# L1 attention with q and k kept transposed, two heads at a time, in a four-layer kernel

## The reference

```python
proj = x @ W_in.T + b_in                       # 256 -> 3 x 16 heads x 64
q, k, v = split(proj)                          # [b, 16, 512, 64] each
q, k = _rope(q, sin, cos), _rope(k, sin, cos)  # lo*cos + hi*sin | hi*cos - lo*sin
att = softmax(causal(einsum('bhqd,bhkd->bhqk', q, k) / 8))
y = einsum('bhqk,bhkd->bhqd', att, v)
return y.reshape(b, t, 1024) @ W_out.T + b_out
```

## Time and profile before

| | us |
|---|---|
| median of 3 runs (lowest to highest) | 2312.48 (2310.83 to 2312.55) |
| the profiled execution, its own time | 2315.66 |
| its span, first to last instruction | 2313.9 |
| PE busy | 1965.5 |
| DVE / ACT / POOL busy | 1723.1 / 1398.9 / 1036.8 |
| L1 attention, its first x transpose to its last update of x | about 949 to 2002 |

### The profile page before, as it was taken

One profiled execution on the slowest core, in us unless ns is written; L12 is line 12 of the kernel. 1 busy time (PEld: TensorE's weight loads), 2 busy tenths in 40 slices (PEclk: granted clock), 3 DMA queues, 4 the chain that ended last, 5 costly groups with the idle time before them and its releaser, 6 DMA issues. The chain is left out here.

```text
span 2313.9 us, 52728 instructions
## 1 busy us (share of the span) xinstructions
PE 1965.5 (85%) x18758; PEld 1405.2 (61%) x18759; DVE 1723.1 (74%) x3717; ACT 1398.9 (60%) x2736; POOL 1036.8 (45%) x1231
## 2 busy tenths in 40 slices
PE   2889989899862999378799999999999999549999
PEld 1666666666561666145577777676767777426665
DVE  4778888788791444468678787879696977679997
ACT  1666666666562444267668696868787878344443
POOL 4435534355014000488747576657575663132222
PEclk9999999999955999689999999999999999869999
DMA  7000000000033332002100000000000000100000
GB/s 241 2 1 2 2 2 2 2 2 2 3 128 127 98 91 79 12 11 35 22 1 2 2 2 2 2 1 2 1 2 2 2 2 2 38 1 14 18 18 23
DMA packets 53114, 57.77 MB, mean 25 GB/s; under 512 B 7121, under 2 KB 47217, under 8 KB 52897
## 3 DMA queue, kind: packets, MB, share of 16 engines
q1 hardware_dynamic: 46240, 45.00, 6.2%
q0 software_dynamic: 6656, 9.85, 2.0%
HBM read 36.22 MB, written 18.61 MB: 24 GB/s over the span
## 5 line engine op out<-in xcount | busy, mean ns | idle before, releaser
L371 PE MATMUL a_bank<-w_in_sb,xnT_sb 128*128 128x512 f16 x1152 | 293.7, 394 | 33.7 <-DVE t_buf_sb L579 26.4
L1116 DVE TENSOR_REDUCE neg_max_sb<-a_bank 128x1 f32<-128x128 f32 (+3 forms) x512 | 236.1, 485 | 92.6 <-PE a_bank L896 88.7
L531 DVE TENSOR_REDUCE neg_max_sb<-a_bank 128x1 f32<-128x128 f32 (+3 forms) x512 | 236.1, 482 | 92.6 <-PE a_bank L288 91.1
L1039 ACT ACTIVATE probT_sb<-a_bank 128x512 f32<-128x512 f32 (+1 forms) x384 | 198.8, 526 | 145.3 <-PE a_bank L919 140.5
L442 ACT ACTIVATE p_hi_sb<-a_bank 128x384 f16<-128x384 f32 (+1 forms) x384 | 205.3, 535 | 120.7 <-PE a_bank L297 119.0
L434 ACT ACTIVATE prob_sb<-a_bank,neg_max_sb 128x128 f32<-128x128 f32 (+3 forms) x512 | 261.4, 543 | 23.9 <-DVE neg_max_sb L531 23.0
L538 DVE TENSOR_TENSOR p_lo_sb<-a_bank,p_hi_sb 128x384 f16<-128x384 f32 (+1 forms) x384 | 228.0, 595 | 59.7 <-ACT p_hi_sb L442 56.1
L453 ACT ACTIVATE stack_sb<-a_bank 128x1024 f16<-128x1024 f16 (+1 forms) x256 | 211.4, 826 | 7.0 <-PE a_bank L342 6.6
L297 PE MATMUL a_bank<-ident_f_sb,prob_sb 128*128 128x128 f32 x1280 | 206.4, 276 | 3.7 <-DVE p_lo_sb L538 3.1
L707 POOL TENSOR_TENSOR rope_w_sb<-t_buf_sb,sin_sb 128x256 f32<-128x256 f32 x128 | 146.0, 1140 | 134.7 <-DVE t_buf_sb L579 132.2
L371 PEld LDWEIGHTS a_bank<-w_in_sb,xnT_sb 128*128 128x128 f16 x1152 | 104.9, 100 | 143.0 <-DVE t_buf_sb L579 34.2
(11 more groups left out here) (268 smaller groups left out, 5613.3 us busy)
## 6 DMA issues: line engine op xcount, KB each, us to landing
sorted_rows<-zeros_sb SPq DMA_DIRECT2D x1, 4992.0 KB, 21.6
x_in_sb<-sorted_rows SPq DMA_DIRECT2D x39, 128.0 KB, 2.1
sorted_results<-y_moe_sb SPq DMA_DIRECT2D x39, 128.0 KB, 1.7
x_sb_sb<-L_attn_x SPq DMA_DIRECT2D x8, 512.0 KB, 10.7
w_raw_sb<-L_ffn_gate_bank SPq DMA_DIRECT2D x8, 512.0 KB, 3.6
w_raw_sb<-L_ffn_up_bank SPq DMA_DIRECT2D x8, 512.0 KB, 4.7
w_raw_sb<-L_ffn_down_bank SPq DMA_DIRECT2D x8, 512.0 KB, 5.8
out<-x_sb_sb SPq DMA_DIRECT2D x32, 128.0 KB, 1.7
```

Of the source, the lines that this page charges most:

```text
L371: last = pe.matmul(out, xnT[:, x, c, j * P:(j + 1) * P], w["in"][:, w_, c, cols], start=k == 0, stop=k == len(terms) - 1)
L531: last = dve.tensor_reduce(neg_max[:, i:i + 1], S[(3 * h + g) % 2][:, off:off + L], AX.X, ALU.max, negate=True)
L1039: act.activation(probT[:, (h // 4) % 2, h % 4, T_AT[r]:T_AT[r + 1]], ST[(3 * h + r) % 2][:, 0:T_AT[r + 1] - T_AT[r]], ACT.Exp).then_inc(s_ ...
L1116: last = dve.tensor_reduce(neg_max[:, h % 2, i:i + 1], S[(3 * h + g) % 2][:, off:off + L], AX.X, ALU.max, negate=True)
```

## The change

`attention` is replaced for L1 by `attention1`. The q and k products are made transposed (weights stationary, tokens moving), so that a unit of 128 rows holds one pair of heads: head 2p in rows 0 to 63, head 2p+1 in rows 64 to 127. What follows from it:

- No stack transposes and no copies of them (342, 453). A fill `qk` is six matmuls of 512 columns, 16 a batch; with 8 `V` fills there are 24 such fills, as before.
- Scores are three products of 64 rows a head (high\*high, high\*low, low\*high) in place of two of 128; those of the two heads alternate, one head writing to bank `S[0]`, the other to `S[1]`. The masks stay products over 128 rows.
- The rotation needs rows exchanged in blocks of 32. SP does it with four SBUF-to-SBUF transfers a pair (`t_buf` to `t_swapped`, 128 KB in all). ACT adds the bias (q and k), DVE makes the cosine part straight from PSUM, POOL the sine part, the sum and the low part, ACT the high part.
- The output projection uses float16 parts: 24 matmuls of 256 columns each in place of eight in float32; DVE makes the low part of yT.
- 24 slots a batch, each with one group of both heads of a pair, and other lags and orders (below). `scores` waits for the exp of both heads of the slot before.

```diff
-LAGS = ((2, 2, 3, 4, 0, 1), (2, 2, 3, 4, 0, 1))
-PE_ORDER = ("STFP", "STPF")
-ACT_ORDER = ("HEW", "PHWE")
-DVE_ORDER = ("OMNWL", "OLWMN")
+AT1 = (tuple(3 * p - 6 for p in range(HEADS // 2)), tuple(3 * p - 5 for p in range(HEADS // 2)),
+       (1, 7, 8, 9), (16, 18, 19, 21), (10, 12, 13, 15), (27, 28, 29, 29), 0)
...
+    LAG_T, LAG_HI, LAG_LO, LAG_PV = 1, 1, 1, 2
+    LAG_WA, LAG_WV, LAG_VH, LAG_VL = 1, 1, 1, 2
+    LAG_W, LAG_ZH, LAG_ZL = (3, 2), (4, 3), (4, 3)
+    LAG_OUT = LAG_PV + 3
+    AT_Q, AT_K, AT_V1, AT_V0, AT_XT, AT_PROJ, YT_LAG = AT1
...
+        out += [("yT", 0, c) for c in range(CHUNKS) if k == 3 * c + LAG_OUT + (c == 0)]
...
+        def scores(b, p, g):
+            G = count(b, 2 * p, g)
...
+            wait(pe, s_exp, G)
+            for i in GROUP_TILES[g]:
+                L = (i + 1) * P
+                for n, (q, k) in enumerate(((z_hi, z_hi), (z_hi, z_lo), (z_lo, z_hi))):
+                    for a in range(2):
+                        rows = slice(a * DH, (a + 1) * DH)
+                        pe.matmul(S[a][:, off:off + L], q[rows, at_q, i * P:(i + 1) * P], k[rows, at_k, 0:L], start=n == 0, stop=False)
+                for a in range(2):
+                    last = pe.matmul(S[a][:, off + L - P:off + L], ident_b[:, :], mask[:, :], start=False, stop=True)
...
+        def fill(b, kind, *a):
+            bank, _ = work_banks.next()
+            if taken[bank]:
+                wait(pe, *taken[bank])
...
+    @block.tensor
...
+        def slot(b, k, last):
+            if k < SLOTS_:
+                scores(b, k // 3, k % 3)
+            for a in range(2):
+                if 0 <= k - LAG_T < SLOTS_:
+                    transpose_probs(b, (k - LAG_T) // 3 * 2 + a, (k - LAG_T) % 3)
+            for a in range(2):
+                if 0 <= k - LAG_PV < SLOTS_:
+                    pv(b, (k - LAG_PV) // 3 * 2 + a, (k - LAG_PV) % 3)
+            for kind, ahead, *a in work(k, last):
+                fill(b + ahead, kind, *a)
...
+    @block.scalar
...
+        def slot(b, k, last):
+            for kind, ahead, *a in work(k - LAG_WA, last):
+                take(kind, b + ahead, *a)
+            for a in range(2):
+                if 0 <= k - LAG_HI < SLOTS_:
+                    hi(b, (k - LAG_HI) // 3 * 2 + a, (k - LAG_HI) % 3)
+                if k < SLOTS_:
+                    exp(b, k // 3 * 2 + a, k % 3)
...
+    @block.vector
...
+        def slot(b, k, last):
...
+            for a in range(2):
+                if k < SLOTS_:
+                    row_max(b, k // 3 * 2 + a, k % 3)
+            for a in range(2):
+                if 0 <= k - LAG_LO < SLOTS_:
+                    lo(b, (k - LAG_LO) // 3 * 2 + a, (k - LAG_LO) % 3)
+            for kind, ahead, *a in work(k - LAG_WV, last):
+                take(kind, b + ahead, *a)
...
+    @block.sync
...
+        for pr in range(B * PAIRS):                  # SP
+            wait(sp, s_t, 2 * pr + 2)
+            wait(sp, s_z, 2 * pr)
+            for r in range(0, P, 32):
+                src = r + 32 if r % 64 == 0 else r - 32
+                sp.dma_start(t_sw[r:r + 32, :, :], t_buf[src:src + 32, :, :]).then_inc(s_sw, 16)
```

More of the change, by code:

```diff
@@ L1296, in load_columns @@
         sp.dma_start(self.w_raw[:, :, cols], d["w_in1"].rearrange("(c p) n -> p c n", p=P)[:, :, cols]).then_inc(self.s_raw, 16)
-        sp.dma_start(self.bias[:, cols], d["L1_attn_b_in"][cols].unsqueeze(0).to_broadcast([P, n])).then_inc(self.s_bias, 16)
+        m = HEADS * DH1 // of
+        sp.dma_start(self.bias[:, bass.ds(i * m, m)],
+                     d["L1_attn_b_in"][bass.ds(i * m + 2 * HEADS * DH1, m)].unsqueeze(0).to_broadcast([P, m])).then_inc(self.s_bias, 16)
     def load_rest(self, sp, d, part):
-        k = HEADS * DH1 // P // 4
-        rest = [(self.w_out[:, part * k:(part + 1) * k, :],
-                 d["w_out1"].rearrange("(c p) n -> p c n", p=P)[:, part * k:(part + 1) * k, :])]
+        rest = []
         if part == 0:
-            rest += [(self.bias_out[:, :], d["L1_attn_b_out"].unsqueeze(0).to_broadcast([P, D]))]
+            rest = [(self.bias_out[:, :], d["L1_attn_b_out"].unsqueeze(0).to_broadcast([P, D])),
+                    (self.bias_qk[:, 0, :], d["b_qk1"])]
         if part > 1:
             t = part - 2
-            rest += [(dst[:, t, :, :], src[t].rearrange("(j p) n -> p j n", p=P))
-                     for dst, src in ((self.cos, d["cos"]), (self.sin, d["sin"]))]
+            rest = [(dst[:, t, :], src[t]) for dst, src in ((self.cos, d["cos"]), (self.sin, d["sin"]))]
         for dst, src in rest:
@@ L1420, in l1_attention @@
     with nc.Block() as block:
-        attention(block, 1, x_sb, stats, consts,
-                  {"in": w_in, "out": l1.w_out, "bias": bias, "bias_out": l1.bias_out, "cos": l1.cos, "sin": l1.sin},
-                  lambda n: sem(n + "_a1"), psb, banks, (act_aside, dve_aside, pool_aside))
+        attention1(block, x_sb, stats, consts,
+                   {"in": w_in, "bias": bias, "bias_qk": l1.bias_qk, "bias_out": l1.bias_out, "cos": l1.cos, "sin": l1.sin}, d,
+                   lambda n: sem(n + "_a1"), psb, banks, (act_aside, dve_aside, pool_aside))
 def load_expert(sp, d, w_raw, s_raw, e):
@@ L2340, in _ @@
                     sp.wait_ge(s_padded, 16)
+            nc.clear_and_free_semaphores(a0_sems)
+            nc.all_engine_barrier()
         with ExitStack() as l1_scope:
@@ L2377, in host_constants @@
     ss = np.concatenate([-sin, sin], -1).astype(np.float32)
-    c["cos"] = np.stack([cc * np.float32(0.125), cc])
-    c["sin"] = np.stack([ss * np.float32(0.125), ss])
+    rows = lambda m, s: np.tile((m * np.float32(s)).T, (P // DH1, 1))
+    c["cos"] = np.stack([rows(cc, 0.125 / W1_SCALE), rows(cc, 1.0 / W1_SCALE)])
+    c["sin"] = np.stack([rows(ss, 0.125), rows(ss, 1.0)])
     return c
@@ L2399 @@
         "gate_wT": t(L0_ffn_gate_w), "w_in1": t(L1_attn_W_in), "w_out1": t(L1_attn_W_out),
+        "b_qk1": np.asarray(L1_attn_b_in)[:2 * HEADS * DH1].reshape(HEADS, P).T,
     }
```

994 lines of the change are left out of this document (407 added, 587 removed).

## The result

The changed kernel takes 2497.47 us (median of 4 runs, 2484.7 to 2502.3), the kernel before 2312.52 (4 runs beside them): the ratio is 1.079, with a 95% interval of 1.0748 to 1.0832. The direction and the mechanism of the forecast of 2404 hold, and the range holds the time, 2.5 us inside its upper end. The size is half of what came: +92 was forecast, +185 measured between the medians, +169.0 between the profiled spans.

The account below looks back on a forecast made before the run. PE was taken to bound the full flow closely; after the change, program order decides. Start -15, batch 0 -15, batches 1 to 6 +104, last batch and tail +17.5, barrier about 1: +92, 2408 profiled, so 2404; range 2340 to 2500.

Parts of the forecast that it names:

- Full overlap: L1 scores: the two heads' 64-row products run at the same time, three terms costing 1.62 us for both, not 3.24.
- The take behind maxima, low parts and exponential: Chain inside an L1 slot: DVE's take of a fill comes last, seen by PE at 3.9 us in g1.
- The slots came out as listed: L1 batch, slots 0 to 23: a time for each, from 3.5 to 9.4 us, sum given as 137.2.
- 140 us a batch: L1 full flow: slots 137.2, plus 0.6 for normalization and 2 for the clock; batches 1 to 6 give +104.
- slot 1: k is free, v waits until 3.9: Slot 1 of a batch: v's fill waits for q's take of slot 0, 3.9 + 1.3 = 5.2 us.
- The clock, where 2 us were given: L1 batch: 2 us added for a clock of 0.99 in full flow, 0.92 in batch 0.
- Batch 0 was set at 131: L1 batch 0: 120 without an earlier batch's projections, 131 with indirect transfers partly on the path, that is -15.
- The start was better than its term: Before L1's first score: four prologue units, transfer round, rotations, v and weight split, about 38 us, that is -15.
- partly on the path: Batch 0: 24 of POOL's 28 indirect transfers lie in slots 10 to 21 and partly delay it, giving 131.
- PE stays the bound: Rival, 12%: takes come when PE wants them, a batch is 117.7 us and the kernel 2250.
- The clock: Rival, 10% for 0.92 or below: PE's waits lower the clock; at 0.92 the time is 2440 to 2450.
- POOL for the transfers: Sign of being wrong: POOL waiting for the row-exchange transfers, which the forecast has hidden.

Follow-up runs that it names:

- the arrangement that removes most waits: Changed kernel with takes between maxima and low parts, last outputs sooner, both high parts first, three normalization steps on GpSimd: 2277.28 us, 0.9852 of the kernel before.

## Why the prediction was right, and where it was short

*Right.* PE's work: 101.1 us a batch forecast, and the arrangement that removes most waits runs a batch in 118.8 with 105.65 busy. Full overlap and the price of a change of part to full array, 0.1, are in the rows above; both heads in one half cost 13.5 to 14.6 a batch where +13 was forecast. The take behind maxima, low parts and exponential stands before each fill: moving it brought some 150 us, and taking the exponential from between the high parts 58. The transfers are hidden. The slots came out as listed, within 0.3 us, for 16 of the 24 (in batch 3 slot 7 is 6.6 for 6.5, slot 16 6.6 for 6.5, slot 22 5.3 for 5.2, slot 23 3.6 for 3.5).

*Short: "140 us a batch" was 150.2*, which is 60 of the missing 77 us (2408 against the 2484.7 of the profiled execution). The others are batch 0 with 29, the last batch with 3, and the start, which gave 15 back. The slots as listed sum to 137.8, not 137.2; a batch took 12.4 more, where 2.6 were given:

- Slots 1 to 3, 5.8 us. The step that failed is "slot 1: k is free, v waits until 3.9" and the two after it. At the start of a batch every engine also runs the last steps of the batch before. The values of slot 2 wait for the outputs of the last pair, which VectorE takes a slot later than PE wants them: 3.6 us a batch, not in the list. Making them a slot sooner brought 24 us in all. The 1.9 of slot 1 and the 1.8 of slot 3, in which the clock is down too, were not tried apart.
- The clock, where 2 us were given. It was 0.94 and not 0.99: four or five times a batch it fell to 1.2 GHz, shortly after waits of PE of 1.9 to 3.6 us. The run that keeps PE busy puts the cost at 4 to 5 us, twice the term. Slots 8, 9, 12, 15 and 18, in or just behind which it is down, are 4.9 longer than listed together in batch 3; in the run that keeps PE busy they are 0.7 longer.
- The other 16 slots are 1.6 longer together, 0.1 each.

*Batch 0 and the start.* Batch 0 was set at 131 and took 152.9, cut at the first scores. Before, so cut, it took 139.3; the window in the earlier trace rows ends 7 us behind it, which made the forecast gain look larger. So -15 was forecast and +13.6 came. The start was better than its term: 30.0 from the first x transpose to the first score, where 38 was given, and the stage began 8.2 earlier, which no term has and whose cause was not looked into (the 1 us given for the barrier is in no row). But the eight us under the term are no gain, they were moved: the prediction put the last value fills and the split of the output weights ahead of the first score, and they ran behind it. VectorE's timeline in slot 0 of batch 0:

```profile
980.92 2.29 DVE L1038 SCALAR_TENSOR_TENSOR w_out_parts_sb<-yT_sb,w_out_parts_sb 128x2048 f16<-128x2048 f32 x1 [2.50 <-ACT w_out_parts_sb L927]
983.13 1.14 DVE L969 TENSOR_REDUCE neg_max_sb<-a_bank 128x1 f32<-128x128 f32 x4
```

The scores began at 970.96, their maxima at 983.13, and slot 0 is 14.2 us long where 4.1 was listed. That is 10 of the 22 us by which batch 0 missed; the term "partly on the path" for the 24 indirect transfers was a guess, and it is not alone in the rest. Slots 7, 8 and 13 are 8.9, 9.0 and 12.2 us long, with GpSimd busy for 113 of 153 us of the batch. In slot 13 VectorE again normalizes beside GpSimd, and the row statistics of a later batch stand behind it, with the maxima last:

```profile
1052.71 1.25 DVE L1026 TENSOR_SCALAR xn_sb<-x_sb_sb,mv_sb,rstd_sb 128x256 f32<-128x256 f32 x1
1053.99 1.36 DVE L1030 CAST xn_part_sb<-xn_sb 128x256 f16<-128x256 f32 x1
1055.39 1.37 DVE L1032 TENSOR_TENSOR xn_part_sb<-xn_sb,xn_part_sb 128x256 f16<-128x256 f32 x1
1056.79 1.37 DVE L1034 TENSOR_TENSOR x_sb_sb<-x_sb_sb,bias_out_sb 128x256 f32<-128x256 f32 x1
1058.08 1.39 DVE L1189 BATCH_NORM_STATS2 bn_sb<-x_sb_sb 128x6 f32<-128x256 f32 x4
```

In the last experiment, with three of these steps on GpSimd, slot 13 of batch 0 is still 11.0: there PE waits 5.6 us for GpSimd's parts, which stand behind the rotation and the indirect transfers. What would cure batch 0 was not tried. *The last batch and tail* took 145.0 for 137.5.

*The rivals.* "PE stays the bound" named its condition rightly, takes that come when PE wants them, and its 2250 is nearly reached once they do (2277, with a batch 0 that is 12 us longer than before, where that sum has it 15 shorter). It was no property of the change but of the order of VectorE's and ScalarE's programs. "The clock" was given as an alternative to the forecast; it is a part of it. Of the signs, a batch of 137 to 143 did not come (150.2), and "POOL for the transfers", a sign of being wrong, came without harm.

## What to carry to other kernels

When a change removes work from the bound engine, write the new program order of the engines that release its buffers slot by slot, batch boundary included: here 5 us less of PE's work a batch came with 33 us more of its waits (the lower clock counted in), and moving a two-line loop gave most of it back. PE's waits also cost clock (0.94 in place of 0.99 here, 4 to 5 us a batch), so they are dearer than their length. After each cure read the waits again, since the next one (the exponentials, then the outputs, then the normalization) was hidden behind the first; and place work beside another engine by the times in the trace, not by slot numbers.

## What the hardware did that was not expected

- Matmuls of 64 rows in different halves of the array are recorded as starting in pairs, 10 ns apart, though the program issues three of one half ahead of those of the other; the time is the same as with alternating order (2490.7 and 2497.5).
- VectorE's steps on operands in SBUF (scale, cast, difference, sum of 128x256) take 1.2 to 1.5 us in place of 0.3 to 0.4 in the rows above, where an operation of GpSimd is under way, and end 0.14 to 0.3 us after it. Maxima, takes and low parts, which read PSUM, keep their lengths beside it (0.74 for the take, 1.01 for two maxima). The Trainium skill, "SBUF — State Buffer", Who interferes with whom, has the rule: a VectorE cast or scale in a two-port mode, or a VectorE instruction with two inputs in SBUF beside a GpSimd one that reads SBUF, can't run at the same time as GpSimd's, and the one that issues first goes first. The rows agree: GpSimd's operation had begun first in each of them, and VectorE's step ends last. That the scale and the cast ran in such a mode is in no record.
